# Rolled loops of five stages of a state-space and attention network written out as straight code

## The reference

```python
x = x + mamba(layernorm(x))            # state-space block: per token h = dA*h + dBu, y = sum_s h*C
x = x + ffn(layernorm(x))              # ternary weights, relu squared, 256 -> 1024 -> 256
x = x + attention(layernorm(x))        # causal, 16 heads of 16, low-rank additions to q and v
x = x + ffn(layernorm(x))
x = x + linear_attention(layernorm(x)) # scores cumulated over the batch axis, no softmax
x = x + moe(layernorm(x))              # 8 experts, 2 of them per token
x = x + mixer_block(layernorm(x))      # a second linear attention with its own feed-forward part
x = x + moe(layernorm(x))
```

## Time and profile before

| | us |
|---|---|
| median of three runs | 3614.89 |
| lowest, highest | 3612.38, 3617.28 |
| the profiled execution | 3592.76 |
| its span, first to last instruction | 3591.0 |

### The profile page before, as it was taken

How to read it: one execution, slowest core, us unless ns; L and a number is a source line. 1 busy time by engine, 2 the same in 40 slices (tenths; PEclk the granted TensorE clock), 3 DMA queues, 4 the chain that set the end, 5 groups by cost and what they waited for, 6 DMA issues and landing times. The chain is left out here.

```text
span 3591.0 us, 53730 instructions
## 1 busy us (share of the span) xinstructions
PE 3129.2 (87%) x16276; PEld 1877.9 (52%) x16277; DVE 2455.6 (68%) x4639; ACT 1664.3 (46%) x3131; POOL 1618.7 (45%) x1645
## 2 busy tenths in 40 slices
PE   6898899889769989897988999979888889998985
PEld 3343344334238744445444488655665677665564
DVE  6999899999977586765848575984338673323335
ACT  5767666667535456574555654322222232223031
POOL 4998889889856422212121164114542000001643
PEclk9999999999999989898998999989999999998997
DMA  4555555455520000000000002701335791000246
GB/s 142 146 140 142 136 140 138 132 140 144 143 60 1 17 1 1 1 2 2 2 2 1 2 1 80 189 1 60 121 120 171 160 121 29 17 12 0 87 134 214
DMA packets 358182, 282.68 MB, mean 79 GB/s; under 512 B 214124, under 2 KB 274320, under 8 KB 357940
## 3 DMA queue, kind: packets, MB, share of 16 engines
q1 hardware_dynamic: 344884, 246.16, 27.2%
q0 software_dynamic: 13056, 33.65, 2.8%
HBM read 205.41 MB, written 76.16 MB: 78 GB/s over the span
## 5 line engine op out<-in xcount | busy, mean ns | idle before, releaser
L715 POOL TENSOR_TENSOR mamba_dBu<-mamba_du,mamba_bcs 128x512 f32<-128x512 f32 x512 | 638.9, 1270 | 100.5 <-DMA mamba_bcs<-mamba_bc 79.7
L634 PE MATMUL mamba_banks<-mamba_hc,ident 128*128 128x512 f32 x1024 | 530.6, 630 | 112.1 <-DVE mamba_hc L953 111.7
L879 ACT ACTIVATE mamba_banks<-mamba_delta,mamba_a_neg 128x512 f32<-128x512 f32 x512 | 351.9, 690 | 182.4 <-DVE mamba_hc L953 169.0
L634 PEld LDWEIGHTS mamba_banks<-mamba_hc,ident 128*128 128x128 f32 x1024 | 179.4, 194 | 419.6 <-DVE mamba_hc L953 304.8
L1802 DVE TENSOR_REDUCE attn_mp<-attn_banks 128x1 f32<-128x512 f32 (+2 forms) x576 | 356.2, 679 | 49.4 <-PE attn_banks L1449 42.5
L953 DVE TENSOR_TENSOR mamba_hc<-mamba_banks,mamba_bcs 128x512 f32<-128x512 f32 x512 | 343.2, 672 | 7.7 <-PE mamba_banks L634 7.6
L946 DVE TENSOR_TENSOR_SCAN mamba_banks<-mamba_banks,mamba_h_end,mamba_dBu 128x512 f32<-128x512 f32 x256 | 326.8, 1277 | 21.0 <-ACT mamba_banks L879 10.3
L946 DVE TENSOR_TENSOR_SCAN mamba_banks<-mamba_banks,mamba_dBu 128x512 f32<-128x512 f32 x256 | 312.1, 1219 | 36.1 <-POOL mamba_dBu L715 20.2
L1446 PE MATMUL attn_banks<-attn_kT,attn_qT 96*128 96x512 bf16 (+3 forms) x768 | 252.9, 364 | 9.5 <-ACT attn_kT L1671 3.7
L1460 PE MATMUL attn_banks<-attn_qT,attn_kT 98*128 98x512 bf16 (+3 forms) x768 | 210.1, 329 | 8.3 <-ACT attn_r L1689 3.8
L1122 POOL TENSOR_TENSOR ffn_hs<-ffn_h,ffn_hs 128x512 fp32r<-128x512 f32 x128 | 162.2, 1296 | 98.7 <-ACT ffn_hs L1151 98.7
(11 more groups left out here) (446 smaller groups left out, 6735.1 us busy)
## 6 DMA issues: line engine op xcount, KB each, us to landing
mamba_bcs<-mamba_bc SPq DMA_DIRECT2D x256, 512.0 KB, 5.0
moe_slots_moe<-moe_pad SPq DMA_DIRECT2D x2, 9252.0 KB, 52.3
moe_xg<-moe_slots_moe SPq DMA_DIRECT2D x144, 128.5 KB, 2.1
mix_qkv<-mixA_qkv SPq DMA_DIRECT2D x8, 1536.0 KB, 6.0
mixA_y<-moe_rows SPq DMA_DIRECT2D x16, 512.0 KB, 5.9
mix_qk<-mix_qkv SPq DMA_DIRECT2D x16, 512.0 KB, 7.8
mix_v<-mix_qkv SPq DMA_DIRECT2D x16, 256.0 KB, 7.3
mix_out<-mixB_oh SPq DMA_DIRECT2D x16, 256.0 KB, 7.5
```

What stands on the lines that cost most here:

```text
L634: pe.matmul(banks[:, SUMS + k % PAIR, :], c.ident[:, :], hc[:, n % RING, :], start=False, stop=True, skip_group_check=True).then_inc(sem(" ...
L715: pool.tensor_tensor(dBu[:, n % RING, :], du[:, v, k, :], bcs[:, i_of(n) % 4, 0, :], ALU.mult)\
L879: act.activation(banks[:, n % RING, :], delta[:, v, k, :], ACT.Exp, scale=a_neg[:, k, st:st + 1])\
```

## The change

In the loops of these stages `Fori` gives way to Python's `range`. The body is emitted once per pass, g is a number, and the counting register, the branch, and the register instructions for waits and addresses are not emitted. Bodies, order, buffers, transfers and peeled groups stay. Later stages keep their loops.

```diff
@@ stage_mamba, group_loop (five engines)
-            with engine.Fori(0, B - 1) as m:
+            for m in range(0, B - 1):
                 group(m * 2 + 1, 1, True, True)
                 group(m * 2 + 2, 0, True, True)
@@ stage_ffn, pairs (called by nobody)
-            with engine.Fori(0, G // 2 - 1) as m:
+            for m in range(0, G // 2 - 1):
@@ stage_ffn: TensorE, POOL, ACT, DVE
-                with pe.Fori(1, G // 2 - 1) as m:
+                for m in range(1, G // 2 - 1):
...
-                with pool.Fori(1, G // 2 - 1) as m:
+                for m in range(1, G // 2 - 1):
...
-                with act.Fori(1, G // 2 - 1) as m:
+                for m in range(1, G // 2 - 1):
...
-                with dve.Fori(1, G // 2 - 1) as m:
+                for m in range(1, G // 2 - 1):
@@ stage_attn: SP, TensorE, POOL, ACT, DVE
-                with sp.Fori(0, B) as b:
+                for b in range(0, B):
...
-                with pe.Fori(1, B) as b:
+                for b in range(1, B):
...
-                with pool.Fori(0, B - 1) as b:
+                for b in range(0, B - 1):
...
-                with act.Fori(1, B) as b:
+                for b in range(1, B):
...
-                with dve.Fori(1, B - 1) as b:
+                for b in range(1, B - 1):
@@ stage_lin, walk (four engines)
-            with engine.Fori(0, (G - 4) // 2) as m:
+            for m in range(0, (G - 4) // 2):
```

## The result

| | before, us | after, us |
|---|---|---|
| median of four runs each | 3615.7 | 3584.18 |
| lowest, highest | 3612.38, 3617.28 | 3580.47, 3586.03 |
| the profiled execution | 3592.76 | 3584.63 |
| its span | 3591.0 | 3582.9 |

The ratio is 0.9913, with a 95% interval of 0.9896 to 0.993: 31.5 us less, where 34.3 less and 3580.6 us were forecast.

What follows compares the result with a forecast made beforehand. The limit changes by stage: DVE in state-space, TensorE in the attention, with losses at taken branches. −13.5 − 17.8 − 3.0 = −34.3 us from 3614.9 gives 3580.6 us (−0.95%); own range 3573 to 3588, full range 3562 to 3602.

Steps and rivals of the forecast that it cites:

- State-space, −13.5 forecast: State-space groups 2 to 5: straight code removes DVE's stops at two pass ends and the later clock loss, −13.5 us.
- Fronts, −17.8 forecast: Attention fronts before sequences 2 and 3: TensorE's stop at its taken branch goes, and the clock's fall with it, −17.8 us.
- The split into 11.1 of stop and 6.7 of clock: Attention fronts: of the 17.79 us excess, 5.6 + 5.5 are TensorE's stops, the remaining 6.7 the fall to 1.2 GHz.
- two blocks: Attention front: two blocks of code taken to lie behind TensorE's 6.95 us idle gap, up to 2.8 us each.
- Heads, −3.0 forecast: Attention heads: register work goes with the loops, −3 us, taken between −3.8 and −2.2.
- DVE's maxima: Attention heads: small DVE operations that free TensorE's banks, named as why register work costs something there.
- Feed-forward, linear attention and the fetching of straight code, 0 forecast: Taken branches there are covered and straight code is fetched ahead: 0; linear attention at most 3.9 us.
- The rival with stops at the blocks of straight code: Unrolled code stops at 23 newly fetched blocks, 2.8 us each: 64 less 34.3, +30, 3645 us; chance 0.05.
- every group takes 18.71 us at full clock: Feed-forward: each group said to take this time whichever part of the code it stands in.
- The rule on branches: All engines: about 108 ns per compare-and-branch, so removing 32 taken branches would be worth 3.5 us at most.
- The branch is not the cause: Rival: the excess belongs to data, clock or memory and recurs; only 3 or 3.5 us go, 3611 us; chance 0.04.
- The 22 us: Whole kernel: timed runs lie this far above the profiled execution, reason unknown; the same difference was assumed after the change.

Runs made afterwards that it cites:

- e1: The kernel before, unchanged, profiled again on chip 2: 3616.17 us, ratio 0.9995.
- e2: The kernel before with only the state-space loop made straight: 3600.98 us, ratio 0.9961.
- e6: The kernel after, but DVE keeps its rolled loops in the state-space stage and the attention: 3597.62 us, ratio 0.9946.
- e4: The kernel after, but TensorE keeps its rolled loops in the state-space stage and the attention: 3592.66 us, ratio 0.9935.
- e3: The kernel before with only the attention's loops made straight, on five engines: 3597.95 us, ratio 0.9949.
- e5: The kernel before with 16 unused semaphore increments on TensorE ahead of its attention, to shift the loop's head: 3613.9 us, ratio 0.999.
- e7: The kernel before with only the feed-forward and linear-attention loops made straight: 3613.84 us, ratio 0.9994.
- e8: All loops of the kernel straight, the later stages' remaining twelve too, where the kernel after keeps those: 3584.55 us, ratio 0.9907.
- e10: The kernel after, but POOL keeps its rolled loop in the attention, on chip 13: 3559.51 us, ratio 0.9906.
- e9: The kernel after, but ACT keeps its rolled loop in the attention, on chip 13: 3560.71 us, ratio 0.9915.

## Why the prediction was right, step by step

**State-space, −13.5 forecast.** Right in size, place and engine. Groups 1 to 6 together are 14.1 us shorter than in the earlier trace rows, 13.0 than in e1; e2 alone gives 14.1 by time. e6 brings the loss back with DVE alone. That TensorE's register work costs nothing here holds: rolled (e4), its groups stay at 118.85 and 120.01. For DVE speak; no run takes its register work away and leaves its stops. DVE's branch has a row of its own at 422.5 us, of 0.06 us; the stop comes behind it, and one instruction packet (q14, at 425.3) falls into it. Its length is not fixed by the code: 3.5 to 5.7 us over the 12 stops in before, e1, e3, e5, e6 and e7.

**Fronts, −17.8 forecast.** Right: −17.0 against the earlier trace rows, −17.5 against e1. e4 puts it on TensorE, e6 takes it off DVE. The split into 11.1 of stop and 6.7 of clock holds roughly. With the stops at 3.9 (e5), or 2.6 over the 1.3 of a straight entry, these fronts are 99.1, some 6 over 93: 2.6 of stop and over 3 that come behind it, at a mean clock of 0.79 where the straight entry has 0.83 to 0.85. With the long stops of the earlier trace rows the same reckoning leaves 3.3 of 8.9 us each. So about 3 us follow from a stop of either length, in which TensorE works at 1.2 GHz after it has stood; over all twelve stops of before, e1, e2, e4, e5 and e7 it is 1.5 to 3.7 us. The prediction took two blocks to lie behind its 6.95 us, and the packets in e5 bear that out. Against the forecast, the front before sequence 2 stays at 94.62, 1.7 to 2.5 over its neighbours, at a clock of 0.82; in e8 it is the last that has 94.62, in e3 95.41. The trace shows where it goes, to a stretch at half clock near the front's start, which the fronts of 92 to 93 us do not have. Its columns are those of the earlier trace rows:

```profile
1608.70:1612.10 3.40, 3.40 (x6) 1.66 (x5) 1.38 (x4) 0.00 (x0) 0.63 (x1) 0.50 0.02 5
```

At half clock 3.4 us of work would take 1.7 at full clock. In the kernel before, such a stretch runs from 1625.0 to 1635.1 us behind the first long stop, in e5 from 1626.4 to 1633.1 behind a short one. Why one straight front meets it and its neighbours do not is open.

**Heads, −3.0 forecast.** The size came out between: −2.1 against the earlier trace rows, −2.7 against e1. Its cause was wrong. The prediction said that DVE's maxima pay for the register work; e6 gives DVE at most 0.06 us per sequence, e4 TensorE nothing, e10 POOL nothing. ACT pays, with 0.6 (e9). That leaves some 0.4 us of the 111.0 in the earlier trace rows that no single engine brings back. It isn't the attention's loops: in e2 and e7, where all five engines keep them, the heads of sequences 1 to 3 are 110.61, 109.90, 110.55 and 109.92, 110.62, 109.87, as with ACT alone in e9 (110.57, 109.86, 110.57). The other part of the spread is a step of up to 0.67 between two forms of the same window, 109.96 and 109.29, and sequence 0 has moved from the short side to the long one although its code was straight in both kernels. The prediction read 109.37 against 111.02 as loops alone; part of that was this step.

**Feed-forward, linear attention and the fetching of straight code, 0 forecast.** Right by e7, and by the groups at 18.71; TensorE's taken branches in these loops last 0.21 to 0.24 us. The rival with stops at the blocks of straight code is excluded: TensorE fetched 8 further packets in groups 3 to 6 without a change in length, and e8, with the most code of all, is as fast. What I had not forecast is the second feed-forward group, 22.75 us before and 21.11 after, in both stages; the prediction's "every group takes 18.71 us at full clock" is wrong for it. It is not the loops: e7 has 21.18 and 21.41, but e3, whose feed-forward is rolled, has 22.78 and 21.10, and e4, with it straight, 21.14 and 22.69. The trace shows the form. Before:

```profile
1070.56 0.19 PEld L1075 LDWEIGHTS ffn_hp<-ffn_ls,ffn_ust 128*128 128x128 f32 x1 [2.56 <-DVE ffn_ls L1198]
1071.83 1.46 PEld L1071 LDWEIGHTS ffn_hp<-ffn_xs,ffn_w1r 128*128 128x128 f32 x4
```

After:

```profile
1057.03 0.19 PEld L1075 LDWEIGHTS ffn_hp<-ffn_ls,ffn_ust 128*128 128x128 f32 x1 [2.46 <-DVE ffn_ls L1198]
1058.28 0.87 PEld L1071 LDWEIGHTS ffn_hp<-ffn_xs,ffn_w1r 128*128 128x128 f32 x4
```

Four loads go from 0.87 to 1.46 us: a stretch at 1.2 GHz (clock 0.58 from 1071.5 to 1074.5), behind an idle time that differs by 0.1 us. It is 1.6 us of chance per stage, won here and lost elsewhere. In the traces of before and after it adds 3.2 us to a gain that the loops did not make.

**The rule on branches.** The Trainium skill, Advanced Engine Details and Errata, § Control Flow Timing, gives a compare-and-branch some 108 ns. The rows here have 40 to 83 ns on any engine when it is not taken, 45 to 74 ns when it is taken on ACT, DVE, POOL and SP, and on TensorE 208 to 243 ns, or 3.3 to 3.9 us in the attention; the measured rows decide. The difference is what the Trainium skill, Runtime: NRT & Kernel Launch, § Instruction fetch mechanics, states, that a taken branch out of the buffered window waits for a transfer; the q8 packet in each short stop of TensorE and the two in each long one agree with it, and so does their absence in e4's state-space stage.

One sentence of the prediction has to be taken back with this, that "the trace shows no branch" (the rival *The branch is not the cause*): the view by source line shows them, and two rows of it would have told beforehand which loops stop TensorE and which do not.

**The 22 us.** I carried them along without a reason. They are in the expert stages (287 and 288 us in the first profile, 296.7 and 300.3 in e1). This did no harm to a forecast made as a difference, and would have spoiled one read from two profiles: 8.1 us for 31.5. The two forms can be told apart in the list of waits (engine, row, releaser: us in total, times, longest) between 2400 and 2660 us. First the kernel after, where the list, like that of e1, names a releaser outside the core's engines:

```profile
DVE x L2605 <- remote: 33.1, 4, 16.1
ACT moe_silu L2518 <- remote: 32.0, 2, 27.6
```

then the first profile of before, where, as in e9, no such entry stands:

```profile
ACT moe_silu L2518 <- PE moe_trp L2404: 46.9, 8, 6.3
DVE x L2605 <- PE moe_yp L2413: 11.8, 14, 2.1
```

What makes the long form is open; I tried nothing on it, since the change does not touch it.

## What to carry to other kernels

Lay windows over equal pieces of work, some entered over a taken branch and some from straight code; their difference is the price of the loop, stops and clock together; here it forecast the gain to 10% (34.3 us against 31.5). Then read the branches' own rows by the loop's source line, and the instruction packets inside a stop. Write out only the loop of the engine that limits the stage, and only where its body is longer than its code buffer: here DVE's in the state-space stage and TensorE's in the attention; by e4, e5 and e6 these two brought nearly all of it, though no run has only these two straight, and ACT's in the attention adds 1.8 us (e9). Where two profiles disagree with the timed runs, compare first the stages that the change does not touch.

## What the runs showed of the hardware

- TensorE's taken branch lasts 0.21 to 0.24 us in the state-space, feed-forward and linear-attention stages (L526, L1103, L1944) and 3.3 to 3.9 us in the attention (L1581), where a packet of its queue starts during it.
- The stop at a taken branch has two sizes for one and the same loop, 6.46 to 7.28 us with two packets inside (before, e1) and 3.52 to 4.10 with one (e2, e4, e5, e7), by where the loop's head lies. In e7 the edit lies in other stages, one of them ahead of this loop. DVE's stop is 3.5 to 5.7 us with one packet, and differs from run to run of the same code.
- In a stage that leans on TensorE, a stop costs some 3 us (1.5 to 3.7) beyond its own length through the clock, whether it is 2.6 or 5.6 us long (e5). In e2 a front loses as much without a stop.
- The loop's register work has a price on ACT, 0.6 us in a window of 110 us, and at most 0.06 on DVE, POOL and TensorE (e4, e6, e9, e10).
- The same kernel takes 25 us less on one chip than on two others, 0.7%. In the traces the two expert stages carry it: 285 to 289 us there, 297 to 303 in the others.
